# Cross-attention and expert FFN in one kernel: prelude and first batch get an order of their own on all engines

## What is computed

```python
Q = (layernorm(x) @ WQ + bQ).reshape(b, 16, -1, 16)
K = (ctx @ WK + bK).reshape(b, 16, -1, 16)      # the reshape mixes tokens and channels
V = (ctx @ WV + bV).reshape(b, 16, -1, 16)
attn = softmax((Q @ K.T) * mask) / 4
x = x + (attn @ V).transpose(...).reshape(b, -1, 256) @ Wp + bp
# FFN: expert 0 has the clean weights, experts 1 to 7 one perturbed copy of them
probs = softmax(h @ Wr + br)                     # h: layernorm(x) * gamma + beta
y_e = gelu(x_n @ W1_e + b1_e) @ W2_e + b2_e      # W1: 256x1024, W2: 1024x256
x = x + probs[0] * y_0 + sum(probs[1:]) * y_1
```

## Time and profile before

| | us |
|---|---|
| median of 3 runs (789.43 to 799.05) | 789.73 |
| the profiled execution's own time | 782.49 |
| its span, first to last instruction | 780.7 |
| busy: PE, DVE, ACT, POOL | 666.9, 520.5, 374.3, 272.1 |

### The profile page before, as it was taken

The page is one execution under the profiler, slowest core; times in us unless marked ns, Lnnn a source line. Parts: engine busy times, 40 slices in busy tenths (PEclk is TensorE's granted clock), DMA queues, the critical chain, the costliest instruction groups (busy, mean ns, idle before and its releaser), DMA issues.

```text
span 780.7 us, 15474 instructions
## 1 busy us (share of the span) xinstructions
PE 666.9 (85%) x5554; PEld 606.4 (78%) x5554; DVE 520.5 (67%) x1210; ACT 374.3 (48%) x472; POOL 272.1 (35%) x288
## 2 busy tenths in 40 slices
PE   2613586799999949999999999999929999999996
PEld 2503476688998939988998988888828888988886
DVE  2824556869979886988979969643895554434543
ACT  1311331583874825584683875754404444354442
POOL 2600323438458435837648455345710000000000
PEclk9855576599999969999999999979978999999998
DMA  4791133154173243064073153112202211222221
GB/s 158 160 181 37 51 59 78 55 110 79 55 164 59 96 81 80 29 154 89 28 164 75 77 119 72 64 54 101 82 1 82 82 38 61 64 81 81 81 54 27
DMA packets 132880, 63.62 MB, mean 81 GB/s; under 512 B 105696, under 2 KB 123104, under 8 KB 132832
## 3 DMA queue, kind: packets, MB, share of 16 engines
q1 hardware_dynamic: 132832, 62.99, 33.0%
HBM read 35.69 MB, written 23.09 MB: 75 GB/s over the span
## 4 chain that ended last, share of the span: by engine, by line
PE 68%; DVE 17%; SPq 6%; issue 4%; DMA 2%; POOL 1%; ACT 1%; DVEq 0%; ACTq 0%; POOLq 0%
PE ps_m L615 8%; PE ps_l L347 7%; PE ps_y L347 7%; PE ps_y L348 6%; PE ps_y L349 6%; PE ps_l L349 6%; PE ps_l L348 6%; PE ps_m L691 4%; PE ps_s L603 4%; PE ps_s L587 4%; DVE region_b L1256 3%; PE ps_s L347 2%; DVE ind L1281 2%; PE ps_s L349 2%; PE ps_s L348 2%
## 5 line engine op out<-in xcount | busy, mean ns | idle before, releaser
L915 ACT ACTIVATE region_b<-ps_l,bias 128x512 f32<-128x512 f32 x128 | 88.0, 688 | 172.1 <-PE ps_l L349 170.1
L347 PE MATMUL ps_y<-w_hi,region_c_hi 128*128 128x256 f32 x512 | 147.6, 288 | 0.0
L348 PE MATMUL ps_y<-w_lo,region_c_hi 128*128 128x256 f32 x512 | 145.4, 284 | 0.0
L349 PE MATMUL ps_y<-w_hi,region_c_lo 128*128 128x256 f32 x512 | 144.8, 283 | 0.0
L347 PE MATMUL ps_l<-x2s_hi,w_hi 128*128 128x512 f32 x256 | 108.6, 424 | 15.5 <-DVE x2s_lo L1140 14.7
L1077 POOL TENSOR_TENSOR region_c_lo<-region_b,region_c_hi 128x512 fp32r<-128x512 f32 x64 | 93.7, 1469 | 67.2 <-ACT region_c_hi L918 67.2
L1587 DVE TENSOR_TENSOR region_c_lo<-region_b,region_c_hi 128x512 fp32r<-128x512 f32 x64 | 44.3, 692 | 96.4 <-ACT region_c_hi L918 95.8
L349 PE MATMUL ps_l<-x2s_hi,w_lo 128*128 128x512 f32 x256 | 102.8, 402 | 0.0
L348 PE MATMUL ps_l<-x2s_lo,w_hi 128*128 128x512 f32 x256 | 102.8, 401 | 0.0
L1051 POOL TENSOR_TENSOR region_a<-region_a,mx 128x1024 f32<-128x1024 f32 x32 | 61.4, 1920 | 116.6 <-DVE mx L1182 116.6
L918 ACT ACTIVATE region_c_hi<-ps_l,bias 128x512 fp32r<-128x512 f32 x128 | 87.5, 684 | 25.2 <-PE ps_y L349 25.2
(11 more groups left out here) (170 smaller groups left out, 1240.8 us busy)
## 6 DMA issues: line engine op xcount, KB each, us to landing
qs<-q_scr SPq DMA_DIRECT2D x16, 512.0 KB, 6.4
acc_scr<-acc SPq DMA_DIRECT2D x8, 514.0 KB, 4.9
acc<-acc_scr SPq DMA_DIRECT2D x8, 514.0 KB, 3.4
xa<-in_x SPq DMA_DIRECT2D x8, 512.0 KB, 5.1
q_scr<-qn_hi SPq DMA_DIRECT2D x16, 256.0 KB, 4.6
q_scr<-qn_lo SPq DMA_DIRECT2D x16, 256.0 KB, 4.8
x<-in_x SPq DMA_DIRECT2D x32, 128.0 KB, 3.7
xt_scr<-region_b SPq DMA_DIRECT2D x8, 512.0 KB, 2.6
```

The costliest lines, as they stand in the source:

```text
L347: eng.matmul(out_ap, a[0], b[0], start=first, stop=False)
L348: eng.matmul(out_ap, a[0], b[1], start=False, stop=False)
L349: return eng.matmul(out_ap, a[1], b[0], start=False, stop=last)
L915: act.activation(g[:, f % 4, :], ps_l[:, f % 2, :], ACT.Gelu_apprx_tanh, bias=bias[:, e, f:f + 1]).then_inc(s["gelu"].handle, 1)
```

## The change

The calls of `body` begin with `body(1)`, and what `body(0)` did is written out in the prelude in another order (`first` is gone). The parts:

1. **Two issue queues.** ACT issues the loads of the context, WK, bK, WV and bV, half of the key loads of the first pair, the high halves of batch 0's queries and first keys, half of its `kbd`, and the key stores of batches 1 to 3. The rest stays with SP.
2. **Context in halves.** Keys are made, biased, stored, reloaded, turned and split by pairs of 128-row blocks (four batches). Batch 0's part of `kh_scr` is stored alone, before the queries are loaded back; batches 4 to 7 come after the loads for batch 1. The mask of batch 0 is loaded with the weights. Keys' staging is in `on` and `acc`.
3. **b1 and b2** are loaded as ten rows (`brow`) and turned by PE into `ps_y`.
4. **PSUM.** `turn_probs(0, j)` and the queries of batch 1 use `ps_y`; `turn_output`, `project` and `turn_x2` of batch 0 use `ps_l`. Both banks have no FFN work yet.
5. **Engines.** The casts of projection weights go from DVE to ACT, the first two normalisations of x from POOL to ACT, and POOL makes the low parts of W1 and W2 in eight pieces in place of two.
6. **Order.** x of batch 1 is normalised and its queries made ahead of the first scores. The scores of batch 1 stand between the late steps of batch 0.

The diff, cut. SP:

```diff
+            sp.wait_ge(k_biased, 2 * pair + 2)
+            sp.dma_start(k_scr.rearrange("b t d -> (b t) d").rearrange("(k p) d -> p k d", p=P)[:, 2 * pair:2 * pair + 2],
+                         kvk[:, 2 * pair:2 * pair + 2]).then_inc(k_out[pair], 16)
...
-            sp.dma_start(bias[:, 0, 0:FC], b1.rearrange("(c p) -> p c", p=P)).then_inc(ld_b, 16)
-            sp.dma_start(bias[:, 0, FC:FC + DC], b2.rearrange("(c p) -> p c", p=P)).then_inc(ld_b, 16)
-            load_row(2, bp)
-            load_w(3, Wp)
-            sp.dma_start(b2row[:, 0, :], b2.rearrange("(a d) -> a d", a=1).to_broadcast([P, D])).then_inc(ld_b2row, 16)
+            sp.dma_start(brow[0:FC], b1.rearrange("(c p) -> c p", p=P)).then_inc(ld_b, 16)
+            sp.dma_start(brow[FC:FC + DC], b2.rearrange("(c p) -> c p", p=P)).then_inc(ld_b, 16)
...
-        sp.wait_ge(kv_biased, KC)
-        sp.dma_start(k_scr.rearrange("b t d -> (b t) d").rearrange("(k p) d -> p k d", p=P), kv[:, 0]).then_inc(kv_out, 16)
-        sp.wait_ge(kv_out, 16)
-        for b in range(B):
-            sp.dma_start(kk[CT * (b % 2):CT * (b % 2) + CT, b // 2].rearrange("k (h d) -> k h d", d=DK),
-                         k_scr[b].rearrange("t (c d) -> (t c) d", d=DK).rearrange("(h k) d -> k h d", k=CT)).then_inc(kk_in, 16)
+            load_mask(0)
+        store_keys(0)
         load_x(1)
-        store_queries(0)
+        load_turned_keys(0, 0, 1)
+        for m in range(DC):
+            wait(sp, q_lo, 0, m + 1)
+            sp.dma_start(q_scr[1, 0].rearrange("h d c r -> (d c) h r")[m * P:(m + 1) * P],
+                         qn[1][:, m, :].rearrange("p (h r) -> p h r", r=R).bitcast(F32)).then_inc(q_out.handle, 16)
+        sp.wait_ge(k_lo, 1)
+        for half_rows in range(2):
+            sp.dma_start(kh_scr[0].rearrange("p (n a o k) -> n o p a k", n=2, a=2, o=2)[1, half_rows],
+                         kT[1][HP * half_rows:HP * half_rows + HP, :, 0:CT].bitcast(F32)).then_inc(kh_first, 16)
         load_queries(0)
-        sp.wait_ge(k_lo, 1)
+        sp.wait_ge(kh_first, 64)
         sp.wait_ge(eye_ready, 5)
...
+        sp.wait_ge(v_biased, KC)
+        sp.dma_start(v_scr.rearrange("b t d -> (b t) d").rearrange("(k p) d -> p k d", p=P), kvv[:]).then_inc(v_out, 16)
+        store_keys(1)
+        load_x(2)
+        sp.wait_ge(v_out, 16)
...
+        load_turned_keys(1, 4, 5, 6, 7)
+        store_queries(1)
+        load_row(2, bp)
+        load_residual(0)
+        sp.dma_start(b2row[:, 0, :], b2.rearrange("(a d) -> a d", a=1).to_broadcast([P, D])).then_inc(ld_b2row, 16)
+        load_queries(1)
+        sp.wait_ge(kh_out, 16 * 8)
+        load_context(1)
+        sp.wait_ge(k_lo, 2)
```

PE, ACT, DVE and POOL:

```diff
-        keys_values(0, ps_l)
+        pe.wait_ge(proj_lo[1], 1)
+        project_context(0, 0, ps_l, k_product)
         turn_queries_input(0)
+        pe.wait_ge(ld_b, 32)
+        pe.transpose(ps_y[:, 0, 0:FC + DC], brow[:], ident[0:FC + DC, 0:FC + DC]).then_inc(b_turned, 1)
         pe.wait_ge(proj_lo[0], 1)
         queries(0)
-        keys_values(1, ps_y)
-        pe.wait_ge(kk_in, 16 * B)
-        pe.wait_ge(kv_biased, KC)
...
+        pe.wait_ge(kk_in[0], 64)
+        turn_pair(0, ps_l, kk).then_inc(k_turned, 1)
+        pe.wait_ge(proj_lo[2], 1)
+        pe.wait_ge(b_ready, 1)
+        for pair in range(2):
+            project_context(1, pair, ps_y, v_product)
+        project_context(0, 1, ps_l, k_product)
+        turn_queries_input(1, (q_lo, 0))
+        pe.wait_ge(v_biased, KC)
+        queries(1, ps_y)
...
+        wait(pe, xT_lo, 1)
         scores(0, 0, 0)
         scores(0, 0, 1)
         total(0)
         scores(0, 1, 0)
         scores(0, 1, 1)
+        turn_probs(0, 0, to=ps_y)
+        scores(0, 2, 0)
...
+        pe.wait_ge(route_ready, 1)
+        values(0, 0)
+        turn_probs(0, 1, to=ps_y)
         scores(0, 3, 0)
         scores(0, 3, 1)
-        pe.wait_ge(route_w, 2 * DC)
-        for c in range(DC):
-            mm = pe.matmul(ps_m[:, 0, 0:E], ones[:], bw[:, c, :], start=c == 0, stop=c == DC - 1)
-        mm.then_inc(route_sum, 1)
-        pe.wait_ge(route_ready, 1)
-        def body(i, rnd, first=False, last=False, turn=False):
+        total(1)
+        values(0, 1)
+        turn_probs(0, 2, to=ps_y)
+        pe.wait_ge(kk_in[1], 64)
+        turn_pair(1, ps_l, kk).then_inc(k_turned, 1)
...
+        values(0, 3)
+        total(2)
+        turn_output(0, ps_l)
+        for s in range(3):
+            count(3, s)
+        scores(1, 0, 0, True)
+        scores(1, 0, 1, True)
+        project(0, 0, ps_l)
+        project(0, 1, ps_l)
+        total(3)
```

```diff
+        act.dma_start(ctxt[:], ctx_in.rearrange("b t d -> (b t) d").rearrange("(k p) d -> p k d", p=P)).then_inc(ld_ctx, 16)
...
+        high_pair(0, cT[0], ps_m, ctx_turned, ctx_hi)
+        high_projection(1, wkv[0][:, 0])
+        high_pair(1, cT[0], ps_m, ctx_turned, ctx_hi)
+        high_projection(0, wqp[0][:, 0])
+        normalise(0)
         high_queries_input(0)
...
+        act.wait_ge(k_out[0], 16)
+        for b in (2, 3):
+            act.dma_start(kk[CT * (b % 2):CT * (b % 2) + CT, b // 2].rearrange("k (h d) -> k h d", d=DK),
...
-        high_queries(0)
+        first_queries(0, 0, ps_s, True)
+        high_projection(3, wqp[0][:, 1])
+        first_queries(0, 1, ps_s, True)
+        high_pair(0, kT[0], ps_l, k_turned, k_hi)
+        act.wait_ge(k_hi, 1)
+        for half_rows in range(2):
+            act.dma_start(kh_scr[0].rearrange("p (n a o k) -> n o p a k", n=2, a=2, o=2)[0, half_rows],
+                          kT[0][HP * half_rows:HP * half_rows + HP, :, 0:CT].bitcast(F32)).then_inc(kh_first, 16)
+        normalise(1)
         act.wait_ge(ld_w[1], 16)
         act.activation(w2s[0][:], wraw[:, 1, :], ACT.Copy).then_inc(w_hi, 1)
-        act.wait_ge(k_turned, 1)
-        act.activation(kT[0], ps_l[:], ACT.Copy).then_inc(k_hi, 1)
+        high_queries_input(1)
+        act.wait_ge(kh_first, 64)
+        act.wait_ge(eye_ready, 5)
+        for h in range(H // QG):
...
+        first_queries(1, 0, ps_y)
+        first_queries(1, 1, ps_y)
+        act.wait_ge(k_lo, 1)
+        for n in range(2):
+            for m in range(QG):
+                half_rows = slice(HP * (m % 2), HP * (m % 2) + HP)
+                act.dma_start(kh_scr.rearrange("b p (n m k) -> n m p b k", n=2, m=QG)[n, m][:, 1:4],
+                              kT[n][half_rows, m // 2, CT:4 * CT].rearrange("p (b k) -> p b k", k=CT).bitcast(F32)).then_inc(kh_out, 16)
```

```diff
+        low_projection(1, wkv[0][:, 0], wkv[1][:, 0])
+        low_projection(0, wqp[0][:, 0], wqp[1][:, 0])
+        low_pair(1, cT, ps_m, ctx_hi, ctx_lo)
+        dve.wait_ge(ld_row[0], 16)
+        bias_context(0, kvk, ps_l, bkb, k_product, k_biased)
         low_queries_input(0)
-        split_projection(3, [w[:, 1] for w in wqp])
-        low_queries(0)
-        bias_context(1, ps_y, bvb)
+        dve.wait_ge(b_turned, 1)
+        dve.tensor_copy(bias[:, 0, :], ps_y[:, 0, 0:FC + DC]).then_inc(b_ready, 1)
+        low_projection(2, wkv[0][:, 1], wkv[1][:, 1])
...
+        low_queries(0, ps_s, (0,))
+        wait(dve, x_in, 1)
+        stats(0, 1, xa)
+        low_queries(0, ps_s, (1,))
         keys_of(1)
...
+        dve.wait_ge(route_sum, 1)
+        dve.tensor_tensor(rc[:], ps_m[:, 0, 0:E], brb[:], ALU.add).then_inc(route_ready, 1)
+        low_pair(0, kT, ps_l, k_hi, k_lo)
+        dve.wait_ge(ld_row[1], 16)
+        for pair in range(2):
+            bias_context(pair, kvv, ps_y, bvb, v_product, v_biased)
+        bias_context(1, kvk, ps_l, bkb, k_product, k_biased)
         dve.wait_ge(state_ready, NS + 5)
         dve.wait_ge(key_ready, 6)
+        low_queries_input(1)
         compares(0, 0)
-        dve.wait_ge(k_hi, 1)
-        dve.tensor_tensor(kT[1], ps_l[:], kT[0].bitcast(F32), ALU.subtract).then_inc(k_lo, 1)
+        low_queries(1, ps_y)
         counts(0)
-        dve.wait_ge(ld_route, 64)
-        for c in range(DC):
-            dve.tensor_scalar(bw[:, c, :], wr[:, c, :], bet[:, c:c + 1], None, ALU.mult).then_inc(route_w, 1)
-            dve.tensor_scalar(gw[:, c, :], wr[:, c, :], gam[:, c:c + 1], None, ALU.mult).then_inc(route_w, 1)
+        low_projection(3, wqp[0][:, 1], wqp[1][:, 1])
...
         top_scores(0, 2)
+        dve.wait_ge(k_out[0], 16)
+        dve.wait_ge(k_out[1], 16)
+        counts(1)
+        normalise_output(0, 0)
+        mask_scores(0, 3, 0)
+        mask_scores(0, 3, 1)
+        top_scores(0, 3)
         decide(1)
         compares(2, 0)
-        mask_scores(0, 3, 0)
-        mask_scores(0, 3, 1)
-        dve.wait_ge(route_sum, 1)
-        dve.tensor_tensor(rc[:], ps_m[:, 0, 0:E], brb[:], ALU.add).then_inc(route_ready, 1)
-        wait(dve, x_in, 1)
...
+        normalise_output(0, 1)
+        low_pair(1, kT, ps_l, k_hi, k_lo)
+        for n in range(2):
+            dve.tensor_copy(key[:, 2 + n, :], halfword(wraw[:, n, :], 0)).then_inc(key_ready, 1)
+        normalise_output(0, 2)
+        counts(2)
```

(25 more changed lines are left out.)

367 lines of the change are left out of this document (236 added, 131 removed).

## The result

| | before | after |
|---|---|---|
| median, us | 789.74 (789.43 to 799.05, 4 runs) | 755.88 (750.13 to 758.80, 4 runs) |
| profiled execution, us | 782.49 | 758.23 |
| its span, us | 780.7 | 756.4 |
| first mask on DVE | 69.20 | 51.04 |
| PE's first transposes of body(1) | 151.56 | 119.74 |

The ratio of the times is 0.9535, with a 95% interval of 0.944 to 0.963. The forecast was 751; the median came out 5 us later, within the range.

The account below looks back on a forecast made before the run. SP's queue and its DMAs bind up to the first mask, no single bound follows, and PE sets the pace from body(1). Savings of 18.0 and 20.9 make 39 off the median 789.73: 751 us, range 738 to 770.

Parts of the forecast that it names:

- First mask: Span start to DVE's first mask: it comes at 51.2 us against 69.20, 18.0 us saved.
- Bias loads: SP's queue before the key store: issues of 3.83 and 4.47 us vanish, SP free at some 17, store landed at 25.5.
- The low half of the keys: Key preparation before the first mask: low half ready at 35.3 us, 5.7 after PE's start at 29.6.
- Ahead of 59.92, the largest term: Small first key stores issued at once land at 40.1, so kbd can begin 19.8 us ahead of 59.92.
- Two queues: DMA issues before the first mask: ACT's share alone brings 4 us by halved issue rows; the rest of the 18 is order.
- The queries of batch 1 in front of the scores: PE before the first scores: twelve matmuls, 5.1 us, end at 47.9, counts at 49.4, so scores start at 49.4.
- Second stretch: First mask to body(1), on DVE: 56.4 busy plus 9 idle makes 65.4 us, ending at 116.6 against 155.5; 20.9 us saved.
- Everything after it as before: From body(1) to the end: PE's work is unchanged, so all runs as before, 39 us earlier.
- Packets bind: Rival, DMAs before the first mask: small pieces bind, not issues; urgent transfers land 10.5 us later, time 761; chance 0.14.
- Its own chain: Rival, second stretch: the first batch's own chain keeps DVE's idle 25.9; stretch gives 4, time 768; chance 0.09.
- ACT stalls at its issues: Rival: ACT's 18 DMA issues between activations stall at up to 4.47 us each; 20 us slower, 810; chance 0.04.
- It doesn't do what it says: Rival: a wait in a new place holds PE in order and gives the gain back; within 2%, 785; chance 0.02.

Follow-up runs that it names:

- experiment 2: Changed kernel with the two bias-row loads issued ahead of the 1 MB loads instead of behind them; median 756.3 us, ratio 0.9606 to the kernel before.
- experiment 3: Changed kernel with the W2 load issued behind the first key store and the load of x(1); median 759.2 us, ratio 0.9605 to the kernel before.
- (5): Changed kernel with the keys of batches 0 to 3 stored together ahead of batch 0's kbd loads; 757.1 us, ratio 0.965 to the kernel before.
- (6): Changed kernel with only the context's halves undone, batch 0's keys still stored first; 758.1 us, ratio 0.967 to the kernel before.
- experiment 7: Changed kernel with context halves undone and SP's waits in the old order, two issuing engines kept; 759.9 us, ratio 0.965 to the kernel before.
- (4): Changed kernel with all 23 of ACT's DMA issues moved to SP's queue; 752.4 us, ratio 0.9504 to the kernel before.
- (8): Changed kernel with DVE's two masks of scores (0,2) put ahead of the compares of step 1; 757.7 us.
- Experiment 1: The changed kernel run again, unaltered; 752.3 us, ratio 0.9537 to the kernel before.
- Experiment 10: Changed kernel with 7, 7, 6 and 6 idle matmuls at four TensorE waits of the second stretch; median 749.4 us, ratio 0.9535 to the kernel before.
- experiment 9: Changed kernel with batch 0's probabilities turned in ps_s behind its last mask instead of in ps_y; 756.9 us, ratio 0.964 to the kernel before.

## Why the prediction was right, and where it wasn't

**What bounds, and the total.** Right in kind: what was saved before body(1) was saved at the end, less what the clock took later. Forecast 39, measured 31.8 at body(1), 24.3 in the two profiled executions, 33.9 in the medians. The near hit of the median has help from the odd place of the profiled executions: that of before lay 7.2 below its median, that of after 2.3 above.

**First mask: 51.2 forecast, 51.04 measured, by terms of which some were wrong.** The closeness is in part luck: terms that were off cancel, and the same kernel gave 49.96 in another profile.
- Bias loads "gone, SP free at some 17": wrong. The issue took 5.98 where 3.83 and 4.47 had stood, and the key store went out at 24.64. I had read the stall as the load's own; experiment 2 shows that it belongs to whatever is issued behind W1 and W2. The store's landing was 27.4 instead of 25.5, PE's start 32.4 instead of 29.6. In experiment 3 a store at 21.21 brought nothing, though with W2 moved behind it.
- The low half of the keys (35.3): measured 35.7. Its term of 5.7 was too long by 2.3, as from PE's start it was 3.4, and the two before it were too short by 2.8 together.
- "Ahead of 59.92, the largest term": kbd did go out at 41, but I gave the small stores the weight. Undoing shows where 7 to 8 of the 18 us are. Storing batch 0's keys apart from those of three others is worth 1 to 2 us (5), the halves 5 to 6 (6), the order of queries, values, mask and the other four batches' keys some 2 more (7). The effects needn't add, and the 11 us left after experiment 7 no run undid. It kept both issue queues; one queue with the old order was not run.
- kbd landed at 48.8, 2.4 later than the 46.4 forecast, each load after 5.6 to 6.5 us instead of 2.2. The queries of batch 1 hid that.
- Two queues: I had set them at 4 us by the issue rows; 0.3 to 1.4 measured (4).
- The queries of batch 1 in front of the scores: right. Forecast 49.4 for the scores, measured 49.76. They are why an earlier kbd brings the mask no further (2, 3); but kbd landed only 0.2 to 1.0 us ahead of the scores in the two profiles of the changed kernel, so a later one shows at once (4, 6).

**Second stretch: 65.4 forecast, 72.2 measured; this step failed.** Both figures run from the first mask to DVE's last compares before the loop (51.04 to 123.26). DVE's busy time was 58.9, not 56.4; its idle time 13.3, not 9. Of the busy time, three of the six steps' compares took 3.71, 2.63 and 3.72 instead of 2.07, beside POOL, where in the kernel before one step's had taken 3.87; I had a row for such a stall and left what is added in the idle time. Of the idle time, what I left out was TensorE's clock: I had seen 0.60 granted and priced nothing by it. DVE's longest waits there, in us, times and longest:

```profile
DVE rs L1361 <- PE ps_m L654: 3.6, 3, 1.4
DVE x L1381 <- PE ps_l L357: 2.7, 2, 1.9
DVE region_a L1350 <- PE ps_s L622: 2.3, 3, 1.9
DVE cnt L1472 <- PE ps_m L732: 2.1, 1, 2.1
DVE ps_m L1400 <- PE ps_m L694: 1.5, 1, 1.5
```

Each is a wait for TensorE, and the waits for batch 1's input and queries that I had counted as going (7.7 and 3.0) are gone. To the handover, the profiles give roughly this order: 76.4 us at 0.58 (8), 73.7 at 0.63 (3), 74.2 at 0.65 (the first profile), 72.3 at 0.67 (1, 2 and 4), 69.7 at 0.76 (10). Experiment 10 shows more than the order: there the clock rose through added work alone, and the stretch grew shorter for it. Of the 13.7 us that the stretch gained, only `ps_y`'s part was undone (9); that the early queries of batch 1 brought the rest is argued from those waits, and no run moved them back.

**"Everything after it as before": wrong by 7.5 us in the profiled run.** The period of the loop took 55.1, 56.5 or 58.3 us as the granted clock was 1.00, 0.97 or 0.94, with PE busy for nearly all of it. Experiment 1 had 56.5 where the first profile of the same kernel had 58.4, so 1.9 of the 3.3 lie within what one kernel's executions differ by. What makes the clock fall inside a full period was not found.

**The rivals.** *Packets bind* was half right. In the last 18 us before the first mask the DMA share was 0.94, ACT's kbd loads landed in a median of 6.0 (before, 2.2), an earlier store gained nothing (3) and a second issuing engine next to nothing (4). Its price of 10.5 wasn't paid, as the queries of batch 1 covered it:

```profile
kbd<-kh_scr ACTq DMA_DIRECT2D x4, 32.0 KB, 6.0
```

*Its own chain*: idle 13.3, nearer to my 9 than to 25.9. *ACT stalls at its issues*: did not happen; kbd's four took 2.81, at most 0.81 each, and the longest of its 18 between activations 1.38. *It doesn't do what it says*: no.

## What to carry to other kernels

Before you move work ahead in a stretch where one engine is the longest waited for, read that engine's clock in the same row: here matmuls that nobody reads, put exactly where TensorE waits and no longer than it waits, brought 8 us beside the 34 of the reordering, and 80 of them behind one such wait cost 18 us. When an issue stalls, look at what was issued ahead of it; in experiment 2, moving the stalled one only moved the stall. And price the parts of a reordering by undoing each: the term that moved farthest (kbd, 19 us) was held by several conditions, and the one I would have kept alone was worth 1 to 2; what no such run undid stays argued.

## What I had not expected of the hardware

- The granted clock differs between executions of one kernel in the same place: the same period with the same 555 matmuls took 58.35, 56.48 and 55.37 us at 0.94, 0.97 and 1.00 (the last in experiment 9).
- After TensorE had idled for 11.7 us, in the turn, its next sixteen values took 3.60 us; with 48 matmuls in that gap they took 1.95, and the clock stayed at 1.00 from 228 to 268.
- The load of b1, 4 KB in eight rows, took 5.98 us to issue behind two loads of 1 MB, and 0.42 ahead of them.
- Giving ACT 23 DMA issues, 18 of them between activations, gained 0.3 to 1.4 us for the first mask, and ACT's copy of x(1) came 2.7 us later for it (40.59 instead of 37.93).
